# Layer 1 of a two-layer graph network: 128-edge tiles and one-hot matmuls in place of lanes with scans

## The reference

```python
# layer 0: graph attention, softmax over the edges of each dst, layer norm, residual, layer norm
x = _layernorm(x + _L0_gnn_ref(x, edge_index, edge_attr_16, ...))
# layer 1
concat = jnp.concatenate([nodes[senders], nodes[receivers], edges], axis=-1)   # 64 + 64 + 32
h = jax.nn.relu(concat @ W1 + b1)                                              # 128 wide
messages = h @ W2 + b2
aggregated = segment_sum(messages, receivers) / jnp.maximum(degree, 1.0)[:, None]
x = _layernorm(x + aggregated + (nodes @ Wn + bn))
```

## Time and profile before

| | |
|---|---|
| median of 3 runs | 5635.98 us (5617.39 to 5643.6) |
| span of the profiled execution, first to last instruction | 4755.7 us |
| difference, in which the profile shows no instruction | 880.3 us |
| POOL busy | 3565.7 us (75%) |
| DVE busy | 2619.7 us (55%) |
| PE busy (modelled) | 1308.6 us (28%) |
| ACT busy | 493.5 us (10%) |
| DMA | 622.28 MB, mean 131 GB/s |

### The profile page before, as it was taken

How to read it: one execution, slowest core, us unless ns; L and a number is a source line. 1 busy time by engine, 2 the same in 40 slices (tenths; PEclk the granted TensorE clock), 3 DMA queues, 4 the chain that set the end, 5 groups by cost and what they waited for, 6 DMA issues and landing times. The chain is left out here.

```text
span 4755.7 us, 33914 instructions
## 1 busy us (share of the span) xinstructions
PE 1308.6 (28%) x3363; PEld 660.9 (14%) x3363; DVE 2619.7 (55%) x8568; ACT 493.5 (10%) x1011; POOL 3565.7 (75%) x3558
## 2 busy tenths in 40 slices
PE   7600000000000000000575333333333333333336
PEld 4300000000000000000453111111111111111126
DVE  6545443344433444433774666666666666666645
ACT  4500000000000000000232111111111111111101
POOL 5777777777777777777676777777777777777766
PEclk9855555555555555555555655655665556556655
DMA  3034333333333333333232555555555555555532
GB/s 124 10 112 160 100 105 118 118 117 112 93 118 118 118 118 99 106 118 113 85 121 94 169 171 167 165 170 170 162 170 171 161 170 171 166 166 171 170 104 63
DMA packets 240932, 622.28 MB, mean 131 GB/s; under 512 B 74956, under 2 KB 102543, under 8 KB 221521
## 3 DMA queue, kind: packets, MB, share of 16 engines
q1 hardware_dynamic: 127568, 443.81, 28.2%
q0 software_dynamic: 113280, 177.74, 14.7%
HBM read 328.11 MB, written 293.29 MB: 131 GB/s over the span
## 5 line engine op out<-in xcount | busy, mean ns | idle before, releaser
L525 POOL DMA_INDIRECT edge_arena<-table1s,ix x1568 | 1518.0, 968 | 477.9 <-issue 435.2
L433 POOL DMA_INDIRECT edge_arena<-table,ix x1440 | 1460.5, 1014 | 438.9 <-issue 438.9
L565 PE MATMUL ps<-w1e_bd,edge_terms 128*128 128x512 f32 x784 | 725.1, 1080 | 1264.4 <-DMA edge_terms<-e32g_d 1264.4
L1191 DVE SCALAR_TENSOR_TENSOR edge_arena<-edge_arena,same 128x128 f32<-128x128 f32 x1568 | 542.0, 346 | 263.6 <-issue 189.1
L565 PE MATMUL ps<-we_bd,edge_terms 128*128 128x32 f32 x392 | 93.6, 403 | 1864.1 <-DVE score L1038 1803.8
L1035 DVE TENSOR_TENSOR score<-edge_arena,node_wide 128x128 f32<-128x128 f32 x49 | 14.2, 291 | 1066.0 <-DMA edge_arena<-table,ix 1065.6
L1057 DVE TENSOR_TENSOR_SCAN edge_arena<-wq,edge_arena 128x32 f32<-128x32 f32 x3136 | 586.8, 268 | 1.8
L1197 DVE SCALAR_TENSOR_TENSOR edge_arena<-edge_arena,same 128x128 f32<-128x128 f32 x1568 | 539.7, 344 | 1.5 <-ACT edge_arena L832 1.2
L565 PEld LDWEIGHTS ps<-w1e_bd,edge_terms 128*128 128x128 f32 x784 | 229.0, 322 | 1759.2 <-issue 1759.2
L1209 DVE TENSOR_TENSOR edge_arena<-edge_arena 128x1024 f32<-128x1024 f32 x196 | 240.9, 1229 | 404.5 <-DMA edge_arena<-table1s,ix 404.5
L832 ACT ACTIVATE edge_arena<-edge_arena 128x1024 f32<-128x1024 f32 x196 | 207.0, 1056 | 1800.9 <-DVE edge_arena L1214 1800.9
(11 more groups left out here) (177 smaller groups left out, 1462.5 us busy)
## 6 DMA issues: line engine op xcount, KB each, us to landing
recv_term<-zeros SPq DMA_DIRECT2D x98, 1024.0 KB, 9.1
edge_arena<-recv_term SPq DMA_DIRECT2D x196, 512.0 KB, 4.1
rows<-edge_arena SPq DMA_DIRECT2D x196, 512.0 KB, 5.1
rows<-edge_arena SPq DMA_DIRECT2D x49, 1152.0 KB, 4.4
edge_arena<-table,ix POOLq DMA_INDIRECT x1568
edge_terms<-e32g_d SPq DMA_DIRECT2D x196, 128.0 KB, 4.8
edge_arena<-table1s,ix POOLq DMA_INDIRECT x1568
edge_terms<-e16g_d SPq DMA_DIRECT2D x49, 256.0 KB, 9.2
```

The lines of the kernel that those rows point to most:

```text
L433: pool.indirect_dma_start(G0[slot][:, u, :], None, table0, bass.IndirectOffsetOnAxis(ap=ix[slot][:, u:u + 1], axis=0)).then_inc(gathered0[ ...
L525: pool.indirect_dma_start(G1[slot][:, u, :], None, table1s, bass.IndirectOffsetOnAxis(ap=ix[slot][:, u:u + 1], axis=0)).then_inc(gathered1 ...
L565: return pe.matmul(out_, lhsT, rhs, start=start, stop=stop)
L1191: stt(X[:, u, :], X[:, u - 1, :] if u else Xb[:, C1 - 1, :], same[:, bass.ds(c * C1 + u, 1)], X[:, u, :], ALU.mult, ALU.add).then_inc(dv1, 1)
```

## The change

Layer 0 and its node stage keep their form. In layer 1:

- Edges are taken in order in tiles of 128 (`T` = 1563 tiles), four tiles to a group of 512 (391 groups), nodes in blocks of 128 (`NJ` = 98). A **step** is one pair of group and block that meet: 391 + 98 - 1 = 488 steps. `local` says for each edge of a step its place in the block; `table_row` loads block, ring slots and due chunk of a step into registers.
- Per step, DVE makes one-hots (`hot`), PE transposes them (`turned`), ACT widens both forms to fp32 (`ahead`), PE sums edge term and receiver term of the block (`pre`), DVE adds the gathered sender rows (`hidden`), ACT applies the relu (`relu`), PE sums the rows per node (`aggregate`), and DVE adds that to the block's running sum in SBUF (`gather_up`).
- POOL issues 1563 gathers written out one by one, ring of 8 chunks of 8 tiles. It no longer scatters to `recv_term` nor gathers last rows for layer 1.
- The edge attributes times W1 are computed during the layer 0 sweep (`edge_term` on PE, `edge_out` on ACT, which also issues the stores) and go to DRAM as `terms1`, 102 MB; the zeros for `recv_term` are no longer written. The step tables are made between chunks 24 and 25 of the layer 0 sweep (`PREP_AT`).
- Between node stage and sweep: `table1d` (6.4 MB) is loaded into SBUF, the nodes' own term is made with 100 small operations, stored and read back.
- The end is 14 batches of 7 blocks.

The diff, cut to its core:

```diff
@@ sync, in chunk0
-                for z in range(2):
-                    sp.dma_start(recv_flat[:, bass.ds(c * (2 * ZERO_COLS) + z * ZERO_COLS, ZERO_COLS)],
-                                 zeros[:, :]).then_inc(recv_zeroed, 16)
+                if not (isinstance(c, int) and c + 1 >= K0):
+                    for half in range(2):
+                        sp.wait_ge(term_mm, c * TG + (half + 1) * TG // 2)
+                        sp.dma_start(edge_terms[2 + half][:, :, :],
+                                     e32g[:, bass.ds(c * TG + (TG + half * TG // 2), TG // 2), :]).then_inc(e32_raw[half], 16)
@@ sync, after the layer 0 sweep
+            sp.dma_start(src_d, src_by_tile[:, 0:TILES]).then_inc(src_stored, 16)
+            sp.wait_ge(src_stored, 16)
+            sp.dma_start(src_t[:, :], src_d).then_inc(src1_in, 16)
+            sp.wait_ge(tabs_ready, 1)
+            sp.dma_start(steps_d, steps_new.rearrange("p k c -> p (k c)")).then_inc(steps_stored, 16)
+            sp.wait_ge(steps_stored, 16)
+            sp.dma_start(steps_i, steps_d).then_inc(steps_in, 16)
@@ sync, before and in the sweep
+            sp.dma_start(Rj.rearrange("p (j f) -> p j f", f=HID), block_rows(table1d[0:NJ * P, :])).then_inc(R_in, 16)
+            sp.wait_ge(own_ready, 1)
+            sp.dma_start(rows_own_q, node_wide[:, :]).then_inc(own_stored, 16)
+            sp.wait_ge(own_stored, 16)
+            for c in range(AHEAD):
+                edges(c, c)
...
+            def chunk1(slot, it, c, ended, tiles=CHUNK * GT, load=True, more=True):
+
+                if ended is not None:
+                    sp.reg_alu(sp_due, ended, 1, ALU.max)
+                    sp.wait_ge(h_ready, sp_due)
+                    sp.sem_inc(freed, 1)
...
+                sp.wait_ge(gathered1[slot], it * (16 * CHUNK * GT) + 16 * tiles)
+                sp.sem_inc(landed, 1)
@@ gpsimd
-            def scatter_first(r):
-                for b in range(NC):
-                    pool.indirect_dma_start(recv_term, bass.IndirectOffsetOnAxis(ap=start_ix[r][:, b:b + 1], axis=0),
-                                            PDs[r][:, b, :], None, bounds_check=NE - 1, oob_is_err=False).then_inc(pds_scattered[r], 16)
+            for t in range(T):
+                c, u = divmod(t, CHUNK * GT)
+                if u == 0 and c >= RINGC:
+                    pool.wait_ge(freed, c - RINGC + 1)
+                pool.indirect_dma_start(G1[:, t % (RINGG * GT) * HID:t % (RINGG * GT) * HID + HID], None, table1s,
+                                        bass.IndirectOffsetOnAxis(ap=src_t[:, t:t + 1], axis=0)).then_inc(gathered1[c % RINGC], 16)
@@ tensor
+                for u in range(GT):
+                    last = pe.transpose(turned_ps[i % 2][:, u * P:(u + 1) * P], B16[i % 4][:, u, :], ident16[:, :])
...
+                mm(bank, ident[:, :], E1[:, bass.ds(e, GE)], True, False)
+                pe.wait_ge(A_ready, k + 1)
+                for u in range(GT):
+                    last = mm(bank[:, u * HID:(u + 1) * HID], A32[i % 2][:, u * P:(u + 1) * P], Rj[:, bass.ds(j, HID)], False, u == GT - 1)
...
+                for u in range(GT):
+                    last = mm(ps[:, 4 + i % 4, 0:P], H1[i % 4][:, u * HID:(u + 1) * HID], B32[i % 4][:, u, :], u == 0, u == GT - 1)
@@ vector
+                tt(B16[i % 4][:, :, :], hot_iota, wide(local[:, bass.ds(k * GT, GT)].unsqueeze(2), [P, GT, P]), ALU.is_equal).then_inc(hot_ready, 1)
...
+                tt(H1[i % 4], G1[:, bass.ds(g, GE)], ps[:, 2 + i % 2, :], ALU.add).then_inc(h_ready, 1)
...
+                stt(state, state, keep[:, bass.ds(k, 1)], ps[:, 4 + i % 4, 0:P], ALU.mult, ALU.add).then_inc(agg_done, 1)
```

More of the change, by code:

```diff
@@ L274, in build, with table_row @@
         COLS = [(c, min(BANK, LANE + 1 - c)) for c in range(0, LANE + 1, BANK)]
+        def table_row(engine, at, n):
+            _, vals = nc.values_load_multi_w_load_instructions(
+                steps_i[0:1, bass.ds(at * 4, n * 4)], engines=(engine,), min_val=0, max_val=NJ * P,
+                skip_runtime_bounds_check_because="block, slot and count of a step, all built on the chip in these bounds")
+            tops = (NJ - 1) * P, (EDGE_RING - 1) * GE, (RINGG - 1) * GE, CHUNKS
+            return [[nc.s_assert_within(v, 0, top, skip_runtime_bounds_check_because="as above: block, ring slot, chunk")
+                     for v, top in zip(vals[4 * i:4 * i + 4], tops)] for i in range(n)]
         @block.sync
@@ L861, in _ @@
+            for b in range(BATCHES):
+                squares(b)
+                if b:
+                    root1(b - 1)
+            root1(BATCHES - 1)
         @block.vector
```

727 lines of the change are left out of this document (455 added, 272 removed).

## The result

The changed kernel takes 5858.44 us (median of 5; 5844.92 to 5916.09), the kernel before 5635.98: **1.0441 times as long, 95% interval 1.0399 to 1.0482**. The prediction said 5544 us, in a range from 5455 to 5790, and faster.

A forecast was written before the change was run, and what follows sets the result against it. It took POOL's rate of issuing gathers to bound both sweeps. Its terms, 5 - 27 + 0 - 6 + 25 + 0 - 89 = -92 us, took the median from 5635.98 to 5544 us, range 5455 to 5790.

The forecast's parts named there:

- layer 0 sweep: Layer 0's gather loop: added matmuls, copies, stores and table building are mostly hidden; +5 us, from 0 to +15.
- seam and node stage: Between the two sweeps: shorter turns without scatters, layer 1 gathers start earlier; -27 us, from -40 to -10.
- start of the sweep: Layer 1's first steps: loads and small operations ahead of them are hidden by POOL's ring; 0, up to +30 us.
- gathers of the sweep: POOL in layer 1: five gathers fewer, -6 us; gathers held by DVE's wide operations, +25 us, from -37 to +236.
- compute in the sweep: Layer 1's steps on PE, DVE and ACT keep just within POOL's pace to the end; 0 us.
- end: After layer 1's last gather: 82 us in place of 171; -89 us, from -100 to -70.
- The gathers under `hot`: Layer 1: gathers meet DVE's one-hot operation with chance 0.45, held 0.28 us each; 61 us over 488 steps.
- Rival B: Layer 1 sweep: `hot` always meets a gather, 273 us instead of 61; kernel 5756 us, slower; chance 0.08.
- A step of 3.4 us: Layer 1 sweep: 3.1 us a step at full clock, 3.4 with register loads of about 1.5 us.
- The register loads: Layer 1, every four steps: 16 registers on PE, 24 on DVE, side by side; about 1.5 us, bounds 0.5 to 6.
- Rival A: Layer 1 sweep, second half: compute takes over, slower; 5624 to 6320 us; chance 0.14 mild, 0.20 strong.
- The test I had written down: Right: layer 1 gathers 1.25 to 1.30 us apart, no `freed` waits; wrong: long L641 idle, layer 0 sweep over 1915 us.

The follow-up runs named there:

- before_again: The kernel before, unchanged, profiled a second time: 5639.1 us, with a profiled span of 5628.3 us.
- after_fourth: The changed kernel, unchanged, run again beside a version without layer 1's edge terms: 5768.66 us, 1.0199 of the kernel before.
- a_gather1of8: The changed kernel with only one gather of eight issued in the layer 1 sweep: 4714.41 us, 0.836 of the kernel before.
- b_gather1of8: The kernel before with only one gather of eight issued in its layer 1 sweep: 4641.91 us, 0.823 of the unedited kernel before.

## Why the prediction was wrong

**The step that failed** is one sentence of the first part: "I make the sum against the span and add the difference unchanged." It took the missing time for a constant, the same for both kernels. The 880 us stand in the span of every held execution, as idle time of VectorE's and the other queues. The held condition costs the kernel before about 880 us and the changed kernel 1106 to 1199 (5765.7 and 5858.44 against 4659.48). In the profile of the result TensorE's turned one-hots alone reach ScalarE 917 us late in all. That the changed kernel loses more because it has more handovers between engines fits this, but no run varies their number alone. Where the condition is that of the profile, the sum holds, each term within its stated bounds (free profile after, against the free profile before; held against held, result against before_again):

| term | predicted | free, measured | held, measured |
|---|---|---|---|
| ahead of the layer 0 sweep | 0 | -1 | +7 |
| layer 0 sweep | +5 | +8 | +115 (+70 in the set of after_fourth) |
| seam and node stage | -27 | -37 | -40 |
| start of the sweep | 0 | 0 | |
| gathers of the sweep (-6 and +25) | +19 | +21 | |
| compute in the sweep | 0 | 0 | +264 with the gathers |
| end | -89 | -90 | -60 |
| sum | -92 | **-99** | +286 |

- *The layer 0 sweep* is hidden as argued, where free. Held, the same 14 us of matmuls with their copies, stores and loads cost 90 us, though their work fits; the text priced durations and no handovers.
- *The gathers under `hot`.* 271 gathers of the free profile started while L1421 ran, and they lasted 0.24 us more than a median one on average, 66 us; the prediction had 0.45 x 488 = 220 and 0.28, 61 us. The mean of L641 rose to 986 ns from 968. Rival B (always the whole) falls. This bears out the rule that the prediction took from the Trainium skill, "GPSIMD Engine Reference", section 8 (Key points), that GpSimd contends with VectorE's instructions of two SBUF inputs. Such a gather ends 0.82 us after the wide operation, unless it starts in the last 0.13 us of it.
- *A step of 3.4 us* was right: 3.45. So was the clock, between 0.7 and 1.0: 0.92 where free, 0.80 where held.
- *The register loads.* The free profile has them, 16 registers on TensorE and 24 on VectorE:

```profile
L339 DVEq TENSOR_LOAD <-edge_arena x122: 1355/1604/1651, 2578.0 to 4576.0; - x122
L339 PEldq TENSOR_LOAD <-edge_arena x122: 851/1107/3287, 2591.0 to 4578.8; - x122
```

  1.6 and 1.1 us, where 1.5 was taken. That was a choice between bounds of 0.5 and 6 us, so that it came out is in part luck. By 200 ns a register from HBM, which the Trainium skill gives in "Runtime: NRT & Kernel Launch", "Instruction fetch mechanics", they would be 4.8 and 3.2; these come out of SBUF, at 67 and 69 ns a register, and the measurement decides. The prediction's "a step about 3.9" by that rule took the shorter of the two loads; by its own scale (3 us of load, a step of 3.8; 6 us, 4.5) the 4.8 us would have made it about 4.2.
- *Rival A*, compute taking over the sweep, is what the result looks like, and at 5.79 us a step the 5.6 of its strong case is near, though the 6320 us it gave are not. Its reason is another. It had TensorE at 1.2 GHz throughout; the granted clock of the held sweep was 0.80, and of the 2.3 us a step above 3.45, 1.9 (917 / 484) are ScalarE's waits for turned one-hots that were ready.
- *The test I had written down* was met in its wrong half: idle times in front of L641 released by SyncE, a layer 0 sweep over 1915 us. The free profile meets the other half: gathers 1.29 us apart with no wait for `freed`, the first at 2559.7, the last at 4575.6 us, the end 81 us later.

Two things could have been seen blind. The times shown were 5617 to 5644 us, so three executions agreed within 0.5% and the profiled one lay 15 to 16% under all of them: that is another condition, not a constant, and it deserved a rival with a chance of its own. And the chances should have been given for a kernel with some 10700 TensorE matmuls in that sweep and eight handovers a step in the place of one with 768 and a few handovers a chunk, where a queue or a signal may run slower than in the one trace at hand.

## What to carry to other kernels

When the profiled span and the measured times differ by more than a few microseconds, profile again before any sum is made: the missing time may be idle time that this one trace doesn't have, and it needn't be the same for both kernels. Cost a change in handovers as well as in durations: here a kernel of long instruction rows on one engine (before) and one of short steps over four engines (after) are 2% apart one way or 2 to 4% the other, by whether a handover takes 0.1 us or several. An engine that issues indirect DMAs without a pause may have a part in it though no wait names it; take most of its gathers out of a run to see.

## What the runs showed of the hardware

- One chip (number 14 on record) was met in both conditions, with the kernel before at 4755.5 and later at 5646.81 us, and every set of runs was of one condition throughout. What decides it is open; no edit tried here did.
- Where held, up to three gathers issued 1.25 us apart pass nearly without effect in the profile of the result (1 of 154 handovers held). Of those ready in the fourth 16 of 24 are held, from the fifth on 161 of 168. 106 of the 180 are delivered in a pause of GpSimd, up to 3.2 us after its last gather's end, where sixteen had gone before; 74 while it goes on. In the kernel before VectorE's and SyncE's own instructions come 0.70 us apart or a multiple of it in such stretches.
- Where free, 1563 gathers in a row held no handover up, at the same median of 944 ns each.
- Which path is congested isn't shown. That GpSimd's gathers are needed for it is (a_gather1of8, b_gather1of8); whether its being busy would do was tried only where nothing is held.
